# Feed-forward of a decoder layer: half of the activations scaled and split in rows and turned by transposing DMAs

## The reference

```python
h = x2 normalised                                   # 256 wide
h = einsum('btd,hd->bth', h, ternary(W_fc))         # 1024 wide
h = gelu(h)
h = layernorm(h, ln_w, ln_b)                        # over the 1024
x3 = x2 + einsum('bth,dh->btd', h, ternary(W_proj)) # back to 256
```

## Time and profile before

| | |
|---|---|
| median of 3 runs | 2553.18 us (2548.82 to 2554.25) |
| profiled execution | 2553.16 us, span 2551.4 us |
| granted TensorE clock over the span | 0.971 |
| TensorE, VectorE, ScalarE, GpSimd busy over the span | 86%, 80%, 63%, 40% |

### The profile page before, as it was taken

How to read it: one execution, slowest core, us unless ns; L and a number is a source line. 1 busy time by engine, 2 the same in 40 slices (tenths; PEclk the granted TensorE clock), 3 DMA queues, 4 the chain that set the end, 5 groups by cost and what they waited for, 6 DMA issues and landing times.

```text
span 2551.4 us, 70786 instructions
## 1 busy us (share of the span) xinstructions
PE 2195.3 (86%) x29031; PEld 1445.0 (57%) x29031; DVE 2035.5 (80%) x4025; ACT 1604.9 (63%) x2354; POOL 1028.5 (40%) x719
## 2 busy tenths in 40 slices
PE   3668889888888888889888888889865899999999
PEld 1435555555555555555555555555533677777776
DVE  6558888888888888888888888888753688888887
ACT  2356666666666666666666666666532777878876
POOL 2133433443344344434433443343221455555553
PEclk7889999999999999999999999999987999999999
DMA  5266777667677666677766667677431233333332
GB/s 137 46 121 112 127 130 121 123 118 128 118 124 129 122 118 123 122 126 124 124 126 118 118 123 130 120 126 126 80 67 46 67 99 91 82 99 90 82 99 59
DMA packets 450784, 277.01 MB, mean 109 GB/s; under 512 B 299344, under 2 KB 401104, under 8 KB 450512
## 3 DMA queue, kind: packets, MB, share of 16 engines
q1 hardware_dynamic: 447408, 272.77, 56.8%
q10 hardware_dynamic: 3104, 0.34, 0.1%
HBM read 54.87 MB, written 33.55 MB: 35 GB/s over the span
## 4 chain that ended last, share of the span: by engine, by line
SPq 44%; PE 32%; DMA 10%; DVE 6%; issue 4%; ACT 3%; POOL 1%; DVEq 0%; ACTq 0%; POOLq 0%
SPq L593 37%; PE ybk L1355 9%; PE hbk L1379 8%; SPq L599 5%; DMA cross_stk<-cross_negmT 5%; PE tbk L1369 4%; PE product_bank L1024 4%; DMA self_stk<-self_negmT 4%; SPq L643 1%; PE score_bank L946 1%; PE score_bank L966 1%; PE exp_bank L946 1%; PE exp_bank L984 1%; DVE cross_mx L828 1%; PE product_bank L1031 1%
## 5 line engine op out<-in xcount | busy, mean ns | idle before, releaser
L730 ACT ACTIVATE prob<-exp_bank 128x1024 f32<-128x1024 f32 x512 | 523.0, 1021 | 288.2 <-PE exp_bank L984 283.8
L828 DVE TENSOR_REDUCE cross_mx<-score_bank 128x8 f32<-128x1024 f32 x256 | 311.2, 1216 | 138.4 <-PE score_bank L966 138.2
L662 POOL TENSOR_TENSOR xs<-xn,xs 128x1024 f16<-128x1024 f32 x64 | 136.2, 2128 | 686.7 <-ACT xs L757 686.7
L828 DVE TENSOR_REDUCE self_mx<-score_bank 128x8 f32<-128x1024 f32 x256 | 310.3, 1212 | 112.2 <-PE score_bank L966 112.2
L662 POOL TENSOR_TENSOR ahl<-attT,ahl 128x512 f16<-128x512 f32 x128 | 148.0, 1156 | 349.5 <-ACT ahl L735 349.4
L1379 PE MATMUL hbk<-wfcT,ffn_xhl 128*128 128x512 f16 x1024 | 262.2, 379 | 6.4 <-ACT hid L1276 3.6
L1339 DVE SCALAR_TENSOR_TENSOR ghl<-tbk,lnwc,ghl 128x512 f16<-128x512 f32 x256 | 188.0, 735 | 98.1 <-ACT ghl L1270 98.0
L1355 PE MATMUL ybk<-wpT,ghl 128*128 128x256 f16 x2048 | 260.5, 273 | 0.8 <-DVE ffn_y L1324 0.7
L1355 PEld LDWEIGHTS ybk<-wpT,ghl 128*128 128x128 f16 x2048 | 197.9, 98 | 66.0 <-DVE ghl L1339 0.9
L946 PE MATMUL exp_bank<-maskBT,pick 64*128 64x512 bf16 x1024 | 155.4, 382 | 74.6 <-ACT prob L730 35.4
L1270 ACT ACTIVATE ghl<-tbk,lnwc 128x512 f16<-128x512 f32 x256 | 174.0, 681 | 67.7 <-PE tbk L1369 67.7
(11 more groups left out here) (159 smaller groups left out, 4642.6 us busy)
## 6 DMA issues: line engine op xcount, KB each, us to landing
self_stk<-self_qk SPq DMA_DIRECT2D x768, 64.0 KB, 2.4
cross_stk<-cross_qk SPq DMA_DIRECT2D x768, 64.0 KB, 2.4
self_src<-in_x SPq DMA_DIRECT2D x32, 512.0 KB, 5.7
ctx_in<-in_ctx SPq DMA_DIRECT2D x32, 512.0 KB, 6.3
x_scratch<-xn SPq DMA_DIRECT2D x32, 512.0 KB, 5.5
ffn_src<-x_scratch SPq DMA_DIRECT2D x32, 512.0 KB, 3.8
out<-ffn_y SPq DMA_DIRECT2D x32, 512.0 KB, 3.6
self_stk<-self_negmT SPq DMA_DIRECT2D x64, 128.0 KB, 3.9
```

Of the source, the lines that this page charges most:

```text
L662: nc.gpsimd.tensor_tensor(out, src, hi, ALU.subtract).then_inc(lo_ready, 1)
L730: act.activation(prob[:, p % 3], ebank[:, :, :], ACT.Exp, scale=EXP_SCALE).then_inc(b.exp_done, 1)
L828: dve.tensor_reduce(a.mx[:, 8 * m:8 * m + 8].rearrange("p (j r) -> p r j", r=2), sbank[:, :, :].rearrange("p r (j k) -> p r j k", j=4), AX ...
```

## The change

Of the 8 slices of a group's activations, 0 to 3 go as before: TensorE turns them, ScalarE and VectorE scale and split them out of PSUM. Slices 4 to 7 (columns 512 to 1023 of `hid`) are no longer turned by TensorE. GpSimd multiplies them in place by ln_w, batch by batch (`scale`: 128 x 512 fp32, four in a round, the fourth at the start of the next round). ScalarE writes the fp16 high half of two batches at a time into `rows` (`high_pair`: 128 x 1024, at the end of step 7 and in step 1 of the next round), VectorE the low half (`low_pair`, in step 0 and at the end of step 2 of the next round), and SyncE's queue turns both halves of a pair in one transposing DMA of 128 x 2048 fp16 into `gd`, two in a round. The second product reads slices 4 to 7 from `gd`, and waits for both DMAs before slice 4. The term -mean x s2 moves from step 3 to step 5 on ScalarE, and the output DMA of k - 2 goes ahead of the input's transposing DMA. One more load brings ln_w, repeated in each partition, before the first round.

```diff
+        rows = sb("g_rows", [P, 2, 2, TURNED, 2, S], F16)          # TURNED = FT // 2 = 4
+        gd = sb("g_turned_rows", [P, 2, 2, TURNED, 2, S], F16)
+        lnw_rows = sb("ffn_lnw_rows", [P, HF])
...
 # sp_body, before the transposing DMA of n's input
+                for pair in range(2):
+                    if here(k - 1):
+                        sp.wait_ge(pairs_lo, 2 * (k - 1) + pair + 1)
+                        wait(sp, y_mm, 8 * (k - 1))
+                        sp.dma_start(gd[:, pair]..., rows[:, pair]..., transpose=True).then_inc(pairs_turned[pair], 16)
+                    if pair == 0 and here(k - 2):
+                        out_group = out_groups[k - 2]
+                        sp.wait_ge(y_ready, 4 * (k - 1))
+                        sp.dma_start(out_group, y[:, half]).then_inc(stored[half], 16)
...
 # pool_body
+            def scale(k, half, b):
+                if isinstance(k, int) and k == 0 and b == 0:
+                    pool.wait_ge(rows_in, 16)
+                pool.wait_ge(hstats_done, 8 * k + 2 * b + 2)
+                pool.tensor_tensor(hid[:, half, b, HF:], hid[:, half, b, HF:], lnw_rows[:, :], ALU.mult).then_inc(scaled, 1)
...
+                if here(q):
+                    scale(q, 1 - half, G - 1)
                 if here(n):
                     pool.wait_ge(moments, n + 1)
...
+                if here(k):
+                    scale(k, half, 0)
                 if here(n):
                     pool.wait_ge(xhi_ready, n + 1)
                     pool.tensor_tensor(xs[:, LO], xn[:, :, :], xs[:, HI], ALU.subtract).then_inc(xlo_ready, 1)
+                if here(k):
+                    scale(k, half, 1)
                 if here(q):
                     ...                                            # y + xc of q, then xc of n
+                if here(k):
+                    scale(k, half, 2)
...
 # act_body
+            def high_pair(k, half, pair):
+                act.wait_ge(scaled, 4 * k + 2 * pair + 2)
+                wait(act, pairs_turned[pair], 16 * k)
+                act.activation(rows[:, pair, HI], hidden_pair(half, pair), ACT.Copy).then_inc(pairs_hi, 1)
...
-                    if here(q):
-                        act.wait_ge(gT_ready, 8 * q + s + 1)
+                    if here(q) and s < TURNED:
+                        act.wait_ge(gT_ready, TURNED * q + s + 1)
...
+                    if s == 1 and here(q):
+                        high_pair(q, 1 - half, 1)
+                    if s == 7 and here(k):
+                        high_pair(k, half, 0)
...
-                    if s == 3 and here(q):                         # the term -mean x s2
+                    if s == 5 and here(q):
...
 # dve_body
+            def low_pair(k, half, pair):
+                dve.wait_ge(pairs_hi, 2 * k + pair + 1)
+                dve.tensor_tensor(rows[:, pair, LO], hidden_pair(half, pair), rows[:, pair, HI], ALU.subtract).then_inc(pairs_lo, 1)
...
                         hidden_moments(q, 1 - half, G - 1)
+                        low_pair(q, 1 - half, 0)                   # s == 0
...
-                    if here(q):
-                        dve.wait_ge(ghi_ready, 8 * q + s + 1)
+                    if here(q) and s < TURNED:
+                        dve.wait_ge(ghi_ready, TURNED * q + s + 1)
...
+                    if s == 2 and here(q):
+                        low_pair(q, 1 - half, 1)
...
 # pe_body
+                elif t == TURNED:
+                    pe.wait_ge(pairs_turned[0], 16 * (q + 1))
+                    pe.wait_ge(pairs_turned[1], 16 * (q + 1))
...
-                    if here(q):
+                    if here(q) and s < TURNED:                     # the four transposes of a step
...
 # ahead of the first round, on SyncE's queue
+            sp.dma_start(lnw_rows[:, :], ins.lnw[HF:].partition_broadcast(P)).then_inc(rows_in, 16)
```

More of the change, by code:

```diff
@@ L107, in decoder_layer_kernel @@
         att = attention(nc, stack, ins, sh, x2_dram, prep)
-        mlp = ffn(nc, stack, sh, x2_dram, out, att)
+        mlp = ffn(nc, stack, ins, sh, x2_dram, out, att)
         LAST = 2 * (NG + 4)
@@ L1147, in attention, with ffn @@
         return part
-def ffn(nc, program, sh, x2_dram, out, before):
+def ffn(nc, program, ins, sh, x2_dram, out, before):
     x2_groups = x2_dram.rearrange("(n b) s d -> n s b d", b=G)
@@ L1159, in ffn @@
     STEPS = 2 * G
-    TURN_BANK = (0, 1, 2, 0, 1, 2, 0, 1)
+    TURNED = FT // 2
+    TURN_BANK = (0, 1, 2, 0)
     with ExitStack() as stack:
@@ L1178, in ffn @@
         hnmr = sb("hnmr", [P, G])
-        ghl = sb("ghl", [P, 2, FT, T], F16)
+        ghl = sb("ghl", [P, 2, TURNED, T], F16)
         y = sb("ffn_y", [P, 2, G, D])
+        rows = sb("g_rows", [P, 2, 2, TURNED, 2, S], F16)
+        gd = sb("g_turned_rows", [P, 2, 2, TURNED, 2, S], F16)
+        lnw_rows = sb("ffn_lnw_rows", [P, HF])
         held = sb("ffn_held_wait", [P, 2, G + 1])
@@ L1194, in ffn @@
         gT_ready, ghi_ready, glo_ready = sem("gT_ready"), sem("ghi_ready"), sem("glo_ready")
+        rows_in = sem("ffn_rows_in")
+        scaled, pairs_hi, pairs_lo = sem("g_scaled"), sem("g_pairs_hi"), sem("g_pairs_lo")
+        pairs_turned = [sem("g_turned_first"), sem("g_turned_second")]
         shift_ready, base_ready = sem("shift_ready"), sem("base_ready")
@@ L1213, in sp_body @@
                 n = k + 1
+                for pair in range(2):
+                    if here(k - 1):
+                        sp.wait_ge(pairs_lo, 2 * (k - 1) + pair + 1)
+                        wait(sp, y_mm, 8 * (k - 1))
+                        sp.dma_start(gd[:, pair].rearrange("p a t b s -> p (a t b) s"), rows[:, pair].rearrange("p a t b c -> p (a t b c)"),
+                                     transpose=True).then_inc(pairs_turned[pair], 16)
+                    if pair == 0 and here(k - 2):
+                        out_group = out_groups[k - 2]
+                        sp.wait_ge(y_ready, 4 * (k - 1))
+                        sp.dma_start(out_group, y[:, half]).then_inc(stored[half], 16)
                 if here(n):
@@ L1218, in sp_body @@
                                  transpose=True).then_inc(x_turned, 16)
[L1219 to L1222, removed]
                 if here(n) and here(k + 3):
@@ L1256, in pool_body, with hidden_pair @@
                                        ALU.add).then_inc(xc_ready, 1)
+                if here(k):
+                    scale(k, half, 2)
+        def hidden_pair(half, pair):
+            return hid[:, half, 2 * pair:2 * pair + 2, HF:].rearrange("p b (t c) -> p t b c", t=TURNED)
         def act_body(i):
             act = nc.scalar
+            def high_pair(k, half, pair):
+                act.wait_ge(scaled, 4 * k + 2 * pair + 2)
+                wait(act, pairs_turned[pair], 16 * k)
+                act.activation(rows[:, pair, HI], hidden_pair(half, pair), ACT.Copy).then_inc(pairs_hi, 1)
             for half in range(2):
@@ L1273, in act_body @@
                         if s == 0:
-                            wait(act, gT_ready, 8 * (k - 1))
+                            wait(act, gT_ready, TURNED * (k - 1))
+                            wait(act, pairs_lo, 2 * (k - 1))
                             wait(act, hmv_ready, 4 * (k - 1))
                         act.activation(hid[:, half, s // 2, s % 2 * HF:(s % 2 + 1) * HF], hbk[:, s % 2], ACT.Gelu).then_inc(hid_ready, 1)
+                    if s == 1 and here(q):
+                        high_pair(q, 1 - half, 1)
+                    if s == 7 and here(k):
+                        high_pair(k, half, 0)
                     if s in (2, 3) and here(n):
@@ L1349, in second @@
             def second(q, t):
-                pe.wait_ge(glo_ready, 8 * q + t + 1)
+                if t < TURNED:
+                    pe.wait_ge(glo_ready, TURNED * q + t + 1)
+                elif t == TURNED:
+                    pe.wait_ge(pairs_turned[0], 16 * (q + 1))
+                    pe.wait_ge(pairs_turned[1], 16 * (q + 1))
                 for b in range(G):
@@ L1354, in second @@
                     for part in (HI, LO):
-                        last = pe.matmul(ybk[:, b], ghl[:, part, t, b * S:(b + 1) * S], sh.wpT[:, t],
+                        turned = ghl[:, part, t, b * S:(b + 1) * S] if t < TURNED else gd[:, b // 2, part, t - TURNED, b % 2, :]
+                        last = pe.matmul(ybk[:, b], turned, sh.wpT[:, t],
                                          start=(t == 0 and part == HI and b % 2 == 0), stop=(t == FT - 1 and part == LO),
@@ L1363, in pe_body @@
                 for s in range(STEPS):
-                    if here(q):
+                    if here(q) and s < TURNED:
                         if s == 0:
                             pe.wait_ge(hid_ready, 8 * (q + 1))
-                        wait(pe, glo_ready, 8 * q + s - (2 if s > 2 else (5 if s == 2 else 1)))
+                        wait(pe, glo_ready, TURNED * q + (0, -2, -1, 1)[s])
                         for b in range(G):
```

## The result

| | before | changed |
|---|---|---|
| median | 2551.60 us (4 runs, 2548.82 to 2554.25) | 2581.11 us (4 runs, 2574.14 to 2589.01) |
| ratio | | 1.0117, 95% interval 1.008 to 1.0154 |
| profiled execution | 2553.16 us | 2576.20 us |

What follows compares the result with a forecast made beforehand. The prediction took TensorE to bound feed-forward before, and in-order ScalarE-GpSimd work after, 17.06 us plus a 1.2 hold, 18.3 a round. 26.8 + 1 + 2.5 = 30 us on 2553 gave 2583 us, range 2544 to 2622.

Steps and rivals of the forecast that it cites:

- TensorE's saved work is free but worthless: Four steps lose transposes: 1.76 us less TensorE work a round, 15.7 left; GpSimd's chain leaves only 0.37 of 1.74 gained.
- GpSimd's busy time: Four added multiplications, 5.1 us, on top of 9: 14.3 us of a round of 15.7, which would just fit.
- Costs of the added operations: Per instruction in a round: multiplication 1.27 us, ScalarE copy 1.06, VectorE subtraction 1.2; transposing DMA lands after 4.3.
- The ScalarE-GpSimd ring of 17.06: In-order work from the second pair's copy round to itself: ScalarE 6.36 us plus GpSimd 10.70, each round.
- One hold of 1.2: First pair's subtraction enters at the end of xc, delaying GpSimd's next multiplication 1.2 us: 18.3 a round; chance 0.58.
- The rival in which it waits out the chain (19.65): VectorE's first subtraction runs only after batch 3's multiplication: 19.65 us a round, 2622 us in all; chance 0.14.
- The DMA ring of 18.3: From batch 3's end over the second pair's subtraction and DMA to ScalarE's next copy: 18.3 us; later DMA lengthens rounds one for one.
- the first ring: The in-order loop through ScalarE and GpSimd from the second pair's copy: 17.06 us, 18.3 with one hold.
- The sign forecast for the first ring: In the rounds, ScalarE's copy of the second pair should wait for GpSimd's fourth multiplication.
- Sum: 26.8 us by the last round's start, 1 to the last round, 2.5 in it: 30 us on 2553, giving 2583.
- The last term: Last round to last output: 15.2 us with a bare 4.3 us DMA, in place of 12.7: 2.5 us added.

Runs made afterwards that it cites:

- the quarter kernel: Slices 0 to 5 turned by TensorE, only 6 and 7 by rows and DMAs, against the kernel before: 2542.37 us, ratio 0.9921.

## Why the prediction was right, step by step

- *TensorE's saved work is free but worthless*: shown. The round has 15.7 us of it in 18.1, and three quarters of the removed transposes could go back at 0.01 us a round.
- *GpSimd's busy time*: the 14.3 us has a slip, since 5.1 and 9 make 14.1. Nothing rests on it.
- *Costs of the added operations*: multiplication 1.272 us (1.27), copy 1.048 (1.06), subtraction 1.218 (1.2), DMA 4.5 at the median (4.3 assumed), up to 6.0.
- *The ScalarE-GpSimd ring of 17.06*: shown bare at 17.09 once nothing is held.
- *One hold of 1.2*: measured 1.0. With neither the subtractions nor `hnmr` held, the round fell from 18.11 to 17.09. That VectorE gets in at the end of a GpSimd instruction, ahead of the one that is due, came true in all rounds but one (the two multiplications take 3.5 us). In that one the subtraction was issued 0.06 us ahead of xc, and xc took 3.39. The rival in which it waits out the chain (19.65) did not occur. Here GpSimd's rows are longer too, which no row of before could show. The Trainium skill ("SBUF — State Buffer", section "Who interferes with whom") says that the ports the two share are an exclusive lock, and that the order of issue and not the shape decides who blocks. The traces agree on both sides, with VectorE held 2.0 us in the quarter kernel (2.72 for 0.68) and GpSimd 1.0 in the changed one.
- *The DMA ring of 18.3*: its length is right (18.23 and 18.26) and its shape is not. It isn't a ring of one round: it ends at ScalarE's copy and must go once around the first ring to close. So a longer or shorter path changes the round by half as much, not "one for one": `hnmr` freed took 1.1 us off it and 0.51 off the round (17.60 to 17.09). What set the changed kernel's round was the mean of both, 18.11. The sign forecast for the first ring, ScalarE's copy waiting for the fourth multiplication, was seen only once in the changed kernel, because the DMA path brings ScalarE there at nearly the same time; it came in each round once that path was 1.1 us shorter.
- *Sum*: predicted 30 us, measured 28.0 without the attention part's 4.9, which the change doesn't touch: start 2.9 (1.3), rounds 20.0 (25.5, as 18.11 is not 18.3), to the last round -0.5 (1), last round 5.6 (2.5). The median rose by 29.5. That the total comes so near is partly luck: the rounds were over-estimated by 5.5 us and the ends under-estimated by 3.2 together.

The last term was mis-sized. These are the last round's matmuls of the turned rows, and the two windows around their start:

```profile
2563.00 6.31 PE L1412 MATMUL ybk<-wpT,g_turned_rows 128*128 128x256 f16 x32 [3.19 <-DMA g_turned_rows<-g_rows]
```

```profile
2559.00:2563.00 4.00, 0.81 (x9) 0.51 (x7) 0.00 (x0) 0.00 (x0) 2.34 (x1) 0.83 0.96 131
2563.00:2569.30 6.30, 6.30 (x32) 4.27 (x32) 0.00 (x0) 0.00 (x0) 0.00 (x0) 0.57 0.00 0
```

I had the bare DMA in it, but not that 32 matmuls behind a wait of 3.2 us take 6.3 us at a clock of 0.57 instead of the 3.5 they take at 1.00, which is 2.8 of the 3.1 missing. Of the start's 1.6 too few, 0.4 is the load of ln_w (the first input's low half came 0.9 later after the attention part, 0.5 assumed); the rest is open.

## What to carry to other kernels

When work leaves the bounding engine for a half idle one, don't add busy times: ask whether somebody now waits for it, and walk the ring of in-order work once around; that sum (17.06, and 1.0 of hold on top), and not the busy time (14.1), led to the new round. Where two such paths are of nearly equal length, follow each until it comes back to where it began: a path that closes only over the other counts by half. Then look for the longest unbroken stretch of GpSimd, and keep VectorE's instructions with two SBUF inputs out of it: a subtraction of 0.7 us cost 2.7 there and 0.7 in a gap. How much of the work to move is a size to choose: a quarter, with that subtraction moved, gained 1.1%, a half lost 1.2%. Three eighths with the subtraction moved was not tried.

## What the runs showed of the hardware that was not expected

- A held instruction of four elements in each partition (`hnmr`) takes 1.2 us, and being tiny does not exempt it; without the hold it takes 0.12. It was worth 0.5 us of round (17.60 to 17.09).
- VectorE, waiting since before GpSimd's instruction ended, started ahead of GpSimd's next one, though GpSimd otherwise runs such instructions without a gap. It did so in all rounds but one.
- TensorE's granted clock stayed at 1.00 with waits of 1.3 us in each round, and fell to 0.54 behind a wait of 4.5 us (the half with the subtraction moved) and to 0.57 behind one of 3.2 us (the last round of the changed kernel), so that the work that had waited also ran slower.
